# A gated cross-attention layer with a routed expert layer: batch 0 with its own table of maxima windows, and expert blocks of two sizes

## What is computed

```python
x = x + tanh(g_xattn) * attention(layernorm(x), ctx, ctx)   # 16 heads of 8, scale 0.125, softmax over 1601
probs = softmax(layernorm(x) @ router_w.T)                  # 8 experts, the best 2 of each row
cw    = top-2 probabilities, divided by their sum
x = x + tanh(g_ffn) * sum_e cw[e] * (gelu(h @ w1[e].T + b1[e]) @ w2[e].T + b2[e])   # 128 -> 512 -> 128
```

## Time and profile before

| | us |
|---|---|
| median of 3 executions | 1366.27 |
| lowest, highest | 1364.55, 1367.53 |
| the profiled execution: its own time | 1369.44 |
| its span in the trace | 1367.6 |
| front, to the first exponential | 50.4 |
| attention, 16 batches | to 1181 |
| experts, from the first to the last gelu | 1184.1 to 1339.4 |
| reading back and adding | from 1347.0 |

### The profile page before, as it was taken

One profiled execution on the slowest core, in us unless ns is written; L12 is line 12 of the kernel. 1 busy time (PEld: TensorE's weight loads), 2 busy tenths in 40 slices (PEclk: granted clock), 3 DMA queues, 4 the chain that ended last, 5 costly groups with the idle time before them and its releaser, 6 DMA issues.

```text
span 1367.6 us, 37652 instructions
## 1 busy us (share of the span) xinstructions
PE 1304.4 (95%) x13838; PEld 632.2 (46%) x13838; DVE 1162.4 (85%) x2239; ACT 1097.7 (80%) x2170; POOL 550.7 (40%) x1215
## 2 busy tenths in 40 slices
PE   5899999999999999999999999999999999999992
PEld 2334444444444444444444444444444434588881
DVE  7789999999999999999999999999999998354344
ACT  2379898989888898888889898989888889765551
POOL 3033436262626262625253535344444412145442
PEclk7599999999999999999999999999999999999996
DMA  3232121212121212121222122222221210486655
GB/s 113 63 93 79 46 68 50 70 47 71 48 75 47 77 42 82 37 73 46 63 56 63 56 64 61 58 63 59 65 58 36 59 29 2 128 252 201 202 188 202
DMA packets 65762, 109.13 MB, mean 80 GB/s; under 512 B 13660, under 2 KB 36572, under 8 KB 65436
## 3 DMA queue, kind: packets, MB, share of 16 engines
q1 hardware_dynamic: 58804, 94.33, 23.4%
q0 software_dynamic: 4544, 9.45, 2.1%
q10 hardware_dynamic: 2232, 2.96, 0.6%
HBM read 48.81 MB, written 14.64 MB: 46 GB/s over the span
## 4 chain that ended last, share of the span: by engine, by line
PE 78%; DVE 15%; issue 3%; DMA 2%; ACTq 1%; ACT 0%; SPq 0%; POOL 0%; POOLq 0%; DVEq 0%
PE pv L796 28%; PE st L748 14%; PE mxp L770 13%; DVE mx L1501 13%; PE st L1030 5%; PE mxp L1040 5%; PE st L854 4%; PE st L868 3%; PE st L826 1%; PE st L880 1%; DMA arena<-results 1%; PE st L838 1%; PE st L903 1%; PE mxp L1006 1%; PE st L913 1%
## 5 line engine op out<-in xcount | busy, mean ns | idle before, releaser
L1501 DVE TENSOR_REDUCE mx<-mxp 128x2 f32<-128x804 f32 x1024 | 986.1, 988 | 71.3 <-PE mxp L770 59.4
L1069 ACT ACTIVATE arena<-st 128x512 f32<-128x512 f32 (+1 forms) x1664 | 891.9, 595 | 85.1 <-PE st L748 78.8
L796 PE MATMUL pv<-arena 128*32 128x256 f32 x6656 | 533.9, 393 | 0.5 <-ACT pv_sb L1076 0.4
L770 PE MATMUL mxp<-kpack,qpack 48*128 48x402 bf16 x2048 | 464.4, 343 | 24.4 <-DVE mx L1501 15.6
L748 PE MATMUL st<-qpack,kpack 51*128 51x256 bf16 (+1 forms) x3328 | 456.9, 272 | 0.4
L748 PEld LDWEIGHTS st<-qpack,kpack 51*128 51x128 bf16 (+1 forms) x3328 | 200.5, 96 | 208.2 <-ACT arena L1069 113.6
L770 PEld LDWEIGHTS mxp<-kpack,qpack 48*128 48x128 bf16 x2048 | 145.7, 93 | 164.3 <-DVE mx L1501 81.0
L796 PEld LDWEIGHTS pv<-arena 128*32 128x32 f32 x6656 | 131.5, 108 | 176.6 <-ACT arena L1069 90.2
L1205 ACT ACTIVATE arena<-st,bias 128x256 f32<-128x256 f32 x156 | 73.2, 474 | 60.3 <-PE st L1030 39.9
L635 POOL CAST mxs<-nmx 128x8 bf16<-128x8 f32 x64 | 12.2, 191 | 255.2 <-DVE nmx L1509 255.1
L678 POOL DMA_INDIRECT results<-ysb,idx x78 | 74.8, 959 | 90.0 <-PE st L1030 42.2
(11 more groups left out here) (186 smaller groups left out, 942.6 us busy)
## 6 DMA issues: line engine op xcount, KB each, us to landing
kpack<-ksp SPq DMA_DIRECT2D x762, 50.0 KB
arena<-in_ctxT SPq DMA_DIRECT2D x15, 800.5 KB, 4.4
arena<-in_w1T SPq DMA_DIRECT2D x39, 256.0 KB
arena<-in_w2T SPq DMA_DIRECT2D x39, 256.0 KB
qpack<-qsp SPq DMA_DIRECT2D x187, 32.0 KB
xblk<-rows SPq DMA_DIRECT2D x39, 132.0 KB
rows<-in_pads SPq DMA_DIRECT2D x8, 264.0 KB
qpack<-mxT SPq DMA_DIRECT2D x128, 3.0 KB
```

The lines of the kernel that those rows point to most:

```text
L770: eng.matmul(mxp[pair % MX_BUFS][:, rg, 0:WIN], qpack[rows, b % 2, g * JJ + jj, t * P:(t + 1) * P], kpack[rows, b % 2, g * JJ + jj, WSTART ...
L796: ins = eng.matmul(pv[32 * j:32 * j + 32, 0:N], vaug[0:n, b % 2, kt, at:at + 32], pt[0:n, (2 * u + rg) % PT_BUFS, jj * N:(jj + 1) * N], st ...
L1069: eng.activation(pt[0:n, c % PT_BUFS, :], ring[bank_of["S", u, p]][0:n, :], ACT.Exp, scale=SCALE).then_inc(s_exp, 1)
L1501: eng.tensor_reduce(mx[:, tj, w, :], mxp[windows_done % MX_BUFS][:, :, 0:WIN], AX.X, ALU.max).then_inc(s_red, 1)
```

## The change

Five things change.

- **Windows of batch 0.** Batch 0 gets a table of its own: 22 windows before the first unit (FIRST), then one or two in each unit, 68 in all. The other batches keep the old table, and start it 26 windows ahead (LEAD) where it was 30 and more.
- **The front on TensorE.** 28 matmuls of 128 columns that nothing reads (`keep_busy`) come between the values of batch 0 and the first window, and one or two of the same behind most of the windows of group 0. The values of batch 1 are made in halves, two tiles behind a window.
- **The front's queues.** `place_maxima(0)` is shared: ScalarE issues one half, SyncE the other, and SyncE's is moved ahead of 8 of the 12 DMAs of group 2's keys.
- **Expert blocks of two sizes.** 28 blocks of 256 rows and 15 of 128: 71 tiles where there were 78. The first 18 are large, then five rounds of large, small, small, large, small. Rows are rounded up to 128. The plan has three phases in place of two (23 large, 5 large, 15 small); the last two are 37 steps in chunks 48 to 60, three a chunk. The last batch is scattered after blocks 9 to 12, and SyncE waits for plan and scatter before the 20th block in order.
- **Loads.** w1 and w2 of an expert lie side by side and come in one DMA, when the block four earlier is done with w2. There are 8 buffers of rows where there were 5.

```diff
-XS_BUFS, W_BUFS, IDX_BUFS, YS_BUFS, BIAS_BUFS = 5, 4, 8, 4, 4
+XS_BUFS, W_BUFS, IDX_BUFS, YS_BUFS, BIAS_BUFS = 8, 4, 8, 4, 4
...
+ORDER = list(range(LARGE - 2 * MIX))
+for k in range(MIX):
+    at, small_at = LARGE - 2 * MIX + 2 * k, LARGE + 3 * k
+    ORDER += [at, small_at, small_at + 1, at + 1, small_at + 2]
+PHASES = [(0, FULL, SL), (FULL, LARGE - FULL, SL), (LARGE, NBK - LARGE, SS)]
...
-X1_AHEAD, Q1_AHEAD, V1_AHEAD = 1, 2, 8
+X1_AHEAD, Q1_AHEAD, V1_AHEAD, V1_MORE = 1, 2, 8, NMX + 1
+BUSY_FIRST = 28
...
-ROWS_AT, LAST_ROWS_AT = {1: 40, 2: 42, 3: 44}, {9: 0, 12: 1, 15: 2, 18: 3}
-LEAD, SHORT = 30, 7
+ROWS_AT, LAST_ROWS_AT = {1: 40, 2: 42, 3: 44}, {9: 0, 10: 1, 11: 2, 12: 3}
+FIRST, LEAD = 22, 26
...
+FIRST_WINDOWS_AT = ("1000000000000000000000000000000000000000000000000000",
+                    "1121121212121221112111112112111111111121122111211112")
...
-    return LEAD + b * PER_BATCH + ISSUED[2 * r + p] - max(0, SHORT - u // 3)
+    if b == 0:
+        return FIRST + FIRST_ISSUED[2 * r + p]
+    return LEAD + b * PER_BATCH + ISSUED[2 * r + p]
...
+def beside_first(n):
+
+    if n == Q1_AHEAD or n > NMX:
+        return 0
+    return 1 if n in (0, X1_AHEAD) or V1_AHEAD <= n < V1_AHEAD + VCH[0][1] else 2
...
-            pack_keys(0, 2)
-            place_maxima(0)
+            pack_keys(0, 2, range(2))
+            eng.wait_ge(s_mxT, 1)
+            place_half(eng, 0, 0)
+            pack_keys(0, 2, range(2, PARTS))
             pack_keys(0, 3)
             pack_queries(1)
...
                 if i >= W_BUFS:
-                    eng.wait_ge(s_hp, HC * (i - W_BUFS + 1))
-                col = eng.value_load(wcol[0:1, i:i + 1], min_val=0, max_val=(NE - 1) * HID)
-                eng.dma_start(wbuf[:, i % W_BUFS, 0, :], w1T[:, bass.ds(col, HID)]
-                              ).then_inc(s_up[i % W_BUFS], 16)
-                if i >= W_BUFS:
                     eng.wait_ge(s_f2, HC * (i - W_BUFS + 1))
-                eng.dma_start(wbuf[:, i % W_BUFS, 1, :], w2T[:, bass.ds(col, HID)]
-                              ).then_inc(s_down[i % W_BUFS], 16)
+                col = eng.value_load(wcol[0:1, ORDER[i]:ORDER[i] + 1], min_val=0, max_val=(NE - 1) * 2 * HID)
+                eng.dma_start(wbuf[:, i % W_BUFS, :, :].rearrange("p s h -> p (s h)"),
+                              w12T[:, bass.ds(col, 2 * HID)]).then_inc(s_wt[i % W_BUFS], 16)
...
-                if i == FULL:
-                    eng.wait_ge(s_plan, 2)
+                if ORDER[i] == LARGE:
+                    eng.wait_ge(s_plan, 3)
                     eng.wait_ge(s_scl, SCATTERED)
...
+            def keep_busy(times):
+
+
+                for _ in range(times):
+                    eng.matmul(pv[:, 0:D], wk_sb[:, :], wq_sb[:, :], start=True, stop=True)
...
+            keep_busy(BUSY_FIRST)
             for n in range(issued(0, 0)):
                 maximum(*divmod(n, NMX))
+                keep_busy(beside_first(n))
...
-                    eng.matmul(hp[q % HP_BUFS][:, 0:SL], wbuf[:, i % W_BUFS, 0, c * P:(c + 1) * P],
-                               xT[:, i % 2, :], start=True, stop=True).then_inc(s_hp, 1)
+                    n = tiles_of(i) * P
+                    eng.matmul(hp[q % HP_BUFS][:, 0:n], wbuf[:, i % W_BUFS, 0, c * P:(c + 1) * P],
+                               xT[:, i % 2, 0:n], start=True, stop=True).then_inc(s_hp, 1)
...
             copy_maxima(0)
+            eng.wait_ge(s_mxT, 1)
+            place_half(eng, 0, 1)
...
-                elif 48 <= q < 57:
-                    for n in range(2 * (q - 48), min(2 * (q - 47), 17)):
-                        plan_step(1, n)
+                elif 48 <= q < 61:
+                    for n in range(3 * (q - 48), min(3 * (q - 47), 37)):
```

More of the change, by code:

```diff
@@ L121, in windows, with first_values @@
     return [divmod(n, NMX) for n in range(issued(u, p), min(to, GROUPS * NMX))]
+def beside_first(n):
+    if n == Q1_AHEAD or n > NMX:
+        return 0
+    return 1 if n in (0, X1_AHEAD) or V1_AHEAD <= n < V1_AHEAD + VCH[0][1] else 2
+def first_values(n):
+    if V1_AHEAD <= n < V1_AHEAD + VCH[0][1]:
+        return 0, [n - V1_AHEAD]
+    c, half = divmod(n - V1_MORE, 2)
+    if 0 <= c < NV - 1:
+        first, tiles = 2 * half, VCH[c + 1][1]
+        return c + 1, list(range(first, min(first + 2, tiles)))
+    return None
 def rank_at(b):
@@ L183, in ring_banks, with tiles_of, tiles_before, writes @@
     return at
+def tiles_of(i):
+    return SJ if ORDER[i] < LARGE else 1
+def tiles_before(i):
+    return sum(tiles_of(j) for j in range(i))
+def writes(i):
+    return 16 * sum(tiles_of(j) for j in range(i % YS_BUFS, i, YS_BUFS))
 def norm_order():
@@ L278, in build @@
         cnt = sb("cnt", [P, NE], I32)
+        units = sb("units", [P, NE])
+        more = sb("more", [P, NE])
         prow = sb("prow", [P, NE], I32)
@@ L672, in write_block @@
             def write_block(i):
-                for j in range(SJ):
-                    eng.wait_ge(s_ysb, SJ * i + j + 1)
+                for j in range(tiles_of(i)):
+                    eng.wait_ge(s_ysb, tiles_before(i) + j + 1)
                     if j > 0:
@@ L1011, in turn_back @@
                 if i > 0:
[L1012 to L1013 removed]
+                    eng.wait_ge(s_ysb, tiles_before(i))
+                for j in range(tiles_of(i)):
                     ins = eng.transpose(turn[:, j * P:(j + 1) * P], yT[:, i % 2, j * P:(j + 1) * P],
@@ L1632, in weigh @@
                 if i >= YS_BUFS:
-                    eng.wait_ge(s_ys[i % YS_BUFS], 16 * SJ * (i // YS_BUFS))
-                for j in range(SJ):
+                    eng.wait_ge(s_ys[i % YS_BUFS], writes(i))
+                for j in range(tiles_of(i)):
                     eng.tensor_scalar(ysb[:, i % YS_BUFS, j, :], turn[:, j * P:(j + 1) * P],
```

162 lines of the change are left out of this document (101 added, 61 removed).

## The result

The changed kernel took **1378.19 us** (median of 4, 1374.73 to 1385.81) beside 1366.24 (1364.55 to 1367.53) for the kernel before on the same chip: a ratio of 1.0096, interval 1.0052 to 1.0139. It is slower by about 12 us, where 1355.0 was forecast and slower had a chance of 0.07. One correction to the text ahead: the second string of `FIRST_WINDOWS_AT` is mistyped in the quoted diff. The kernel's is `1121121212221112111112112111111111121122111211112112`; the running count of windows by the one shown is never off by more than one. One count of the prediction fits only the mistyped string: 49 windows left in batch 0 behind unit 13, where the kernel's own leaves 48.

A forecast was written before the change was run, and what follows sets the result against it. TensorE was taken to bound later batches, so front and experts could move: -1.8 + 0.8 - 8.4 - 2.0 + 2.0 + 1.0 - 0.8 + 0.3 - 2.4 = -11.3 us. Forecast 1355.0 us, range 1340 to 1364.

The forecast's parts named there:

- The first exponential: Front: batch 0's first exponential on ScalarE at about 44.7 us instead of 50.37, 5.7 us earlier.
- The clock should then be 1.00: Front, TensorE: with 28 idle matmuls hidden in the wait, granted clock 1.00 where it was 0.50.
- The rival that `keep_busy` does not hold the clock: Front: half clock from 23 us as before, `mxT` 1.7 us later, the whole at 1357; chance 0.10.
- The wait at unit 13: Batch 0: TensorE and ScalarE stand 7 to 10 us for late placed maxima; exponential at 75.3, front nets -1.8 us.
- After unit 13 batch 0 has 49 windows by either table: no difference: Rest of batch 0 behind unit 13: same number of windows with either table, so no change in time.
- The groups' maxima come up to 4 us later in every batch: nothing: Every batch, from LEAD 26: maxima up to 4 us later, turns placed 5 to 9 us behind them, no cost.
- The last batch: LEAD 26 moves four windows into the last batch, where VectorE is nearly full: +0.8 us, range 0 to 3.7.
- The experts: Expert stage: 28 blocks at 3.90 us and 15 short ones at 2.3 instead of 39 at 3.90: -8.4 us.
- The plan's +2.0: Expert plan: 37 steps on VectorE in chunks 48 to 60 instead of 17 make it late, cost 0 to 3.8 us.
- The tail: End of the kernel: a short last block leaves GpSimd three writes instead of five: -2.4 us.
- The +1.0 for crowding: Expert weight loads: later starts and a round's 3.55 MB in 14.7 us, between 0 and 5 us over 25 blocks.
- The half-clock rival for slower: Batch 0: the clock stays at half after the stand at unit 13, giving 1385; chance 0.06.

The follow-up runs named there:

- e2: The changed kernel with LEAD back at 30 and four more windows in batch 0 (units 17, 22, 27, 32): 1372.9 us, ratio 1.004.
- e3: The changed kernel with SyncE placing group 1's maxima before batch 1's queries and the weight loads, and some keys packed earlier: 1383.38 us, ratio 1.0103.
- e4: The changed kernel with the edits of e2 and e3 together: 1378.81 us, ratio 1.0085.
- e9: The changed kernel itself, unaltered, run again on a third chip: 1378.76 us, ratio 1.0089 to the kernel before.
- e13: e7 with batch 0's four extra windows at units 34, 37, 41 and 45 instead of 17, 22, 27 and 32: 1350.53 us, ratio 0.9869.
- e6: The changed kernel with 36 idle matmuls before the first window instead of 28: 1367.45 us, ratio 1.0024.
- e11: e7 with LEAD 26 and the change's table of batch 0: 1353.35 us, ratio 0.9907.
- e10: e7 without any idle matmul: 1352.68 us, ratio 0.9907.
- e7: The changed kernel with LEAD 30 and its table, 36 idle matmuls, batch 1's first keys at units 9 to 12, SyncE's queue ordered by need: 1346.88 us.
- e14: e7 with two of the four extra windows later (units 36, 44) and four DMAs of batch 1's first keys issued earlier: 1351.29 us, ratio 0.9918.
- e12: e7 with the expert stage of the kernel before: 1358.37 us, ratio 0.9965.
- e1: The kernel before with only the new expert stage: 1360.11 us, ratio 0.9944.
- e15: e1 again, on a fourth chip: 1361.35 us, ratio 0.9943.
- e8: e7 with the plan of the last blocks at two steps a chunk in chunks 48 to 66: 1346.83 us, ratio 0.9854.
- e16: e14 again, on the first chip: 1350.90 us, ratio 0.9894.

## Why the prediction was wrong

**The first exponential** was right: 44.5 for 44.7, where the clock holds.

**"The clock should then be 1.00"** is the first step that failed. The rival that `keep_busy` does not hold the clock had 0.10; with 28 idle matmuls it holds in the first profile and not in e2, e3, e4 and e9, with 36 in all but e13. That the profiled execution kept the clock was luck: the other three of the result, 3 to 11 us slower, have mean clocks of 0.967 to 0.974, as e9's execution with half clock in front has 0.972. The rival's price failed too: it was put at 1357, as if a slow clock with idle matmuls were the front of before. It is worse, by 8.3 us at the first exponential (58.7 against 50.4), since at 1.2 GHz two of them and a window pair need 1.6 us, more than VectorE's reduction. The rows gave this: at half clock a window pair took 0.59, and twice 0.237 doubled is 0.95; the sum of 1.5 against 0.93 was never made.

**The wait at unit 13** was right in place, cause and size: 8.61 us for 7 to 10, the exponential at 74.6 for 75.3, SyncE's placement at 69.8 for 70.3, half clock behind it. What the prediction did not do was to go on down the queue. "After unit 13 batch 0 has 49 windows by either table: no difference" is the second step that failed: +10.8 us measured for +2.0. The stand is followed by 13.7 us at half clock (67.5 to 81.1), of which only part lies behind unit 13; up to unit 26 the kernel loses 0.5 us. Unit 39 meets the next placement that stands behind 24 packing DMAs (108.66; it was wanted at 108.2), and 13.7 us more at half clock follow (111.9 to 125.5): +2.3 from unit 26 to 39, +7.9 behind it. The queue had been just in time before: group 1's maxima were issued 8.6 us ahead of their first exponential, groups 2's and 3's only 4.0 and 3.2 us (92.81 for 96.85, 110.14 for 113.33), and from such an issue to the first matmul that it releases 2.6 us pass (108.66 to 111.29). So whatever the front gained beyond that had to come back there, not at unit 13 alone. The count of windows was no part of the miss. That the waits and the clock behind them are all of it is shown by e6 and e11, which differ in SyncE's order and the units of the first keys: batch 0 ends at 132.5 in e6 and 114.9 in e11, which takes 50.2 us behind unit 13, as the prediction had it.

The Trainium skill (TensorE: Matmul & The Clock Gate, Part 1) was weighed against this part, with its sentence that the warm-up is under 1% of a typical span. Where no idle matmuls run at the slow clock the runs agree with it: e10's last exponential ends 5.5 us behind e7's, 0.4%. Lost with the idle matmuls in place, the clock costs more: e14's two groups of runs, with the clock kept and lost in front, are 18 us apart (1351 and 1369), 1.3%.

**"The groups' maxima come up to 4 us later in every batch: nothing"** is the third step that failed, and the dearest: +12.3 us for 0. e2 and e7 against e11 show it alone. A batch whose TensorE is busy 70.27 of 70.67 us has no room for reductions that arrive where VectorE has its routing work, though no wait at the placed maxima ever showed. The prediction looked only for that wait. The last batch, where it expected 0.8, got 0.3; in e9 it is 66.6 us for 63.6 before, with 6.9 us at half clock in it.

**The experts** were right in their mechanism and too small: 3.90 and 2.26 for 3.90 and 2.3, -13.7 in this execution and -11.5 by medians (e12) for -10.3; on the chips with late blocks it was -6 to -7 (e1, e15). The plan's +2.0 is nothing where it was tried (e8), and the stall at the late plan was real: e12, on a chip without late blocks, still has one, 5.35 us at the 22nd. The tail gave 1.8 for 2.4. The +1.0 for crowding did not show on the chips without late blocks. Two of the prediction's sums have slips on which nothing hangs: its other estimate of a short block, 1.9 us, would put the sum 5.5 us lower than the 2.3 taken, not 3, and the 5.2 us that the tightest block leaves for its weights are 5.4.

The half-clock rival for slower, priced from 34 us of slow clock on, had the sign and the wrong course: the clock comes back each time, and then falls again at the next wait.

## What to carry to other kernels

A queue that issues in a fixed order has slack only against the present schedule: if its users come 6 us earlier, list every later entry with the time at which it will be wanted, not the first one alone. Filler that keeps an engine's clock up must be priced at the slow clock as well, since that is when it runs if it fails; and a change of lead in a loop that runs 13 times at 99% busy is worth a look at every unit, because 0.9 us there outweighed all that the front could give. More idle matmuls, a reordered queue and the old lead together turned +12 us into -18 (e7 on the second chip) and -15 (e16 on the first); of the -18, 11.5 are the expert stage, which the change had all along.

## What was not expected of the hardware

The same program up to 23 us, on profiles shifted by 1 us, kept a granted clock of 1.00 in one execution and fell to 0.50 in another (the first profile and e9), with 28 idle matmuls and 1.7 us of idle time before the first window in both; with 36, three of ten executions of e14 lay 18 us above the rest, at a mean granted clock of 0.978 for 0.992. In e9, 41 us then passed at half clock although TensorE was busy 17.14 of 18 us from 23 to 41 us.

Four chips gave two kinds of expert stage for one program, 172 and 179 to 182 us, with a stand of ScalarE that begins 2.5 to 3.5 us after a scatter on one kind only, while the kernel before differed by 3 us at most between them (1364.45 to 1367.48).

A packing DMA on SyncE mostly kept its price of 0.65 us (12 in 7.85, 18 in 11.75, 20 in 13.02), but not always: 24 took 15.68 us before and 17.92 after, with two that took 1.1 us more than the rest, which was enough to decide a wait of 2.77. The load behind the ones took 3.05, as before 3.23.
